# A graph layer's segment sum: one TensorE loop with an empty first pass, and a last block whose x and b2 come by products

## What is computed

```python
agg = segment_sum(edge_attr, dst, 6250)        # edge_attr 200000 x 128 fp32, dst sorted
h = relu(concat([x, agg, u[0] for every node]) @ W1 + b1)
y = h @ W2 + b2
out = layernorm(x + y)                         # 6250 x 128, over the 128 features, eps 1e-5
```

## Time and profile before

| what | value |
|---|---|
| median of three runs | 274.97 us (274.71 to 275.29) |
| the profiled execution | 274.97 us |
| its span, first to last instruction | 273.2 us |
| around the span | 1.77 us |
| TensorE / DVE / ACT / POOL busy | 78% / 64% / 19% / 15% |
| moved by DMA | 110.06 MB, mean 403 GB/s |
| mean granted TensorE clock | 0.949 of full |

### The profile page before, as it was taken

One profiled execution on the slowest core, in us unless ns is written; L12 is line 12 of the kernel. 1 busy time (PEld: TensorE's weight loads), 2 busy tenths in 40 slices (PEclk: granted clock), 3 DMA queues, 4 the chain that ended last, 5 costly groups with the idle time before them and its releaser, 6 DMA issues.

```text
span 273.2 us, 15327 instructions
## 1 busy us (share of the span) xinstructions
PE 213.4 (78%) x6767; PEld 168.1 (62%) x6767; DVE 175.8 (64%) x435; ACT 50.8 (19%) x100; POOL 40.9 (15%) x49
## 2 busy tenths in 40 slices
PE   0886899999787886875669899876797976867872
PEld 0774687877655665644557677655476755655751
DVE  7842258698874784687434867779658576465542
ACT  0410022122211211210202322212022212121210
POOL 6400010040210210310300302102004011030020
PEclk9997579999999999999779999999799999999997
DMA  7999999999999999999999999999999999999995
GB/s 245 395 396 400 400 397 404 402 402 405 401 402 403 402 405 408 417 415 418 412 405 419 419 415 418 417 419 417 424 431 423 427 426 422 427 425 421 430 396 200
DMA packets 27327, 110.06 MB, mean 403 GB/s; under 512 B 2008, under 2 KB 3374, under 8 KB 25134
## 3 DMA queue, kind: packets, MB, share of 16 engines
q1 hardware_dynamic: 24052, 105.83, 95.7%
q10 hardware_dynamic: 3258, 4.00, 4.3%
HBM read 106.63 MB, written 3.20 MB: 402 GB/s over the span
## 4 chain that ended last, share of the span: by engine, by line
PE 60%; issue 14%; DMA 13%; DVE 9%; ACT 1%; DVEq 1%; POOL 1%; POOLq 0%
PE rows_ps L868 32%; PE cols_ps L880 15%; DMA slots<-in_edge_attr 13%; PE hid_ps L894 4%; PE hid_ps L912 3%; PE hid_ps L903 3%; PE hid_ps L888 2%; ACT rows L446 1%; DVE z L680 1%; DVE tall_ids L688 1%; DVE first_of_pair L572 1%; DVE hot L617 1%; POOL rstd L410 1%; DVE dst_local L585 1%; DVE high L699 1%
## 5 line engine op out<-in xcount | busy, mean ns | idle before, releaser
L868 PE MATMUL rows_ps<-slots,hot 64*32 64x128 f32 x6240 | 112.5, 284 | 31.7 <-issue 27.5
L868 PEld LDWEIGHTS rows_ps<-slots,hot 64*32 64x32 f32 x6240 | 93.2, 110 | 48.8 <-issue 46.4
L643 DVE TENSOR_TENSOR agg_t<-agg_t,cols_ps 128x128 f32 (+1 forms) x65 | 21.1, 324 | 83.3 <-PE cols_ps L880 81.4
L880 PE MATMUL cols_ps<-row_hot,rows 128*128 128x128 f32 (+1 forms) x260 | 55.2, 337 | 14.3 <-ACT rows L446 7.3
L617 DVE TENSOR_TENSOR hot<-edge_node,iota 128x768 f32<-128x768 f32 x65 | 61.9, 952 | 2.2 <-issue 1.9
L880 PEld LDWEIGHTS cols_ps<-row_hot,rows 128*128 128x128 f32 x260 | 40.5, 199 | 28.3 <-issue 15.1
L446 ACT ACTIVATE rows<-rows_ps 128x256 f32<-128x256 f32 x65 | 24.9, 383 | 176.7 <-PE rows_ps L868 169.6
L410 POOL TENSOR_TENSOR rstd<-var_eps,minus_half 128x4 f32<-128x4 f32 (+1 forms) x13 | 15.8, 1216 | 194.6 <-DVE var_eps L674 194.6
L633 DVE TENSOR_TENSOR row_hot<-row_node,iota 128x256 f32<-128x256 f32 (+1 forms) x65 | 37.5, 576 | 0.0
L401 POOL TENSOR_TENSOR z<-x_rows,b_all 128x512 f32<-128x512 f32 (+1 forms) x13 | 17.3, 1331 | 31.5 <-PE hid_ps L888 31.5
L680 DVE TENSOR_SCALAR z<-z,moments,rstd (+1 forms) x49 | 16.6, 398 | 1.1 <-POOL rstd L410 1.0
(11 more groups left out here) (119 smaller groups left out, 70.8 us busy)
## 6 DMA issues: line engine op xcount, KB each, us to landing
slots<-in_edge_attr SPq DMA_DIRECT2D x65, 1536.0 KB, 16.8
x_rows<-in_x ACTq DMA_DIRECT2D x11, 256.0 KB
out<-z SPq DMA_DIRECT2D x11, 256.0 KB
dst_int<-in_dst ACTq DMA_DIRECT2D x1, 384.0 KB, 4.1
dst_int<-in_dst SPq DMA_DIRECT2D x1, 384.0 KB, 4.6
x_rows<-in_x ACTq DMA_DIRECT2D x1, 192.0 KB
out<-z SPq DMA_DIRECT2D x1, 192.0 KB
rest_slot<-in_edge_attr ACTq DMA_DIRECT2D x1, 128.0 KB, 8.7
```

The lines of the kernel that those rows point to most:

```text
L643: V.tensor_tensor(cols, cols, cols_ps[:, 0:n], ALU.add).then_inc(added, 1)
L868: done = T.matmul(rows_ps[i][c * SPAN:(c + 1) * SPAN, h, 0:feats], hot[j][part, c * RUN + r, :], slots[part, j, c, r * feats:(r + 1) * fea ...
L880: done = T.matmul(cols_ps[:, 0:n], rows[i][:, h, :], row_hot[j][:, h, 0:n], start=(h == 0), stop=(h == HALVES - 1))
```

## The change

TensorE has one loop for all 13 laps. Around it is a loop of two passes; in the first, `real` is 0, the lap loop runs once and every step in it is branched over, as is the preparation (`before_laps`). In every lap `level2(t-1)` comes behind `level1(t)`, but in step 4 of a lap `level2(t-1)` comes ahead of `level1(t)`, for there are only two pairs `rows_ps` and `rows` now. All `row_hot` and all sums but the last step's have 224 columns. The banks set free hold the transposed x and y apart from the hidden sums. The blocks are shifted by 128 nodes: block 0 now has the three pieces, blocks 1 to 11 are whole, and `final` is still the first 128 nodes. In the last lap, ahead of `level1` of step 64, two products place x and b2 of the final block in y's bank, and `product2` of that block adds onto them; DVE takes its statistics from that bank and normalises from there, without `residual`. The product L961 is gone. DVE has one loop for laps 1 to 11; the last lap and the ending stand twice, in the two arms of a branch on the plan, and SP's last store too. POOL clears `x_rows` at the start, and the load of x waits for that. What DVE does in laps 1 to 4 for the last steps' ids (`turn_tall_ids`) is done in laps 3 to 6.

```diff
-SETS = (0, 1, 0, 1, 2)
-DENSE_LAP = 5
-DENSE = DENSE_LAP * LAP
...
+    width = FIRST + chunks * BLOCK
+
+    top_rows = ROWS - 1
+    top_parts = nodes - FIRST - (blocks - 1) * BLOCK - top_rows * P
+    top_even = top_parts // 16 * 16
...
-        rows_ps = [pb(f"rows_ps{i}", [P, HALVES, 512]) for i in range(3)]
+        rows_ps = [pb(f"rows_ps{i}", [P, HALVES, 512]) for i in range(2)]
         cols_ps = pb("cols_ps", [P, 512])
-
+        turn_bank = pb("turn_bank", [P, BLOCK])
         hid_ps = pb("hid_ps", [P, BLOCK])
-        y_ps = hid_ps[:, :].rearrange("p (r f) -> p r f", r=ROWS)
-        turn_ps = y_ps
+        y_bank = pb("y_bank", [P, BLOCK])
+        y_ps = y_bank[:, :].rearrange("p (r f) -> p r f", r=ROWS)
+        turn_ps = turn_bank[:, :].rearrange("p (r f) -> p r f", r=ROWS)
...
             for i in range(final):
                 store(i)
             plan_now = general_if(sp)
-            store(final)
-
...
+            G.memset(x_rows[:, :, :], 0.0).then_inc(x_zero, 1)
...
+
             bias_add(0, 0)
+            bias_add(1, 1)
             for i in range(places):
                 reciprocal_deviation(i, i)
-                if i + 1 < places:
-                    bias_add(i + 1, i + 1)
+                if i + 2 < places:
...
-                    act.dma_start(x_rows[:, 0, :], x_first).then_inc(x_in, 16)
                 else:
-                    act.dma_start(x_rows[:, :, :].rearrange("p r f -> p (r f)"), x_full[blocks - 1 - i]).then_inc(x_in, 16)
+                    act.wait_ge(x_zero, 1)
+                for memory, home in pieces_of(seq % places, x, lambda parts, r0, r1: x_rows[parts, r0:r1, :].rearrange("p r f -> p (r f)")):
+                    act.dma_start(home, memory).then_inc(x_in, 16)
...
                 for j in range(LAP):
                     t = lap * LAP + j
-
-                    if dense_lap:
+                    if t:
                         copy_rows(t)
-                    elif t + 1 < DENSE:
-                        copy_rows(t + 1)
-                    if j == 0 and lap:
-                        relu(lap - 1)
-                    elif j == 3:
+                    if j == 1:
+                        if lap:
+                            relu(lap - 1)
                         copy_x(lap)
-                    elif j == 4 and lap < final:
+                    elif j == 3 and lap < final:
...
-                    with dve.If(t < DENSE):
-                        make_row_hot(t, i, False)
-                    with dve.If(t > DENSE - 1):
-                        make_row_hot(t, i, True)
-                else:
-                    n = DENSE_COLS if dense_step else COLS
-                    V.tensor_tensor(row_hot[i][:, :, 0:n],
-                                    row_node[:, bass.ds(t, 1), :].rearrange("p o h -> p (o h)").unsqueeze(2).broadcast_to([P, HALVES, n]),
-                                    iota[:, 0:n].unsqueeze(1).broadcast_to([P, HALVES, n]), ALU.is_equal).then_inc(row_hot_made, 1)
-
...
-                        if j == 2:
-                            residual(lap - 1, lap - 1)
-                        elif j == 3:
-                            variance(lap - 1, lap - 1)
-                        elif j == 4:
-                            normalise(lap - 1, lap - 1)
-                    make_hot(t + AHEAD, j + AHEAD, None if mixed else False)
-                    if not isinstance(lap, int) and j in turned_at:
+                    if j == 0 and looped:
+                        with dve.If(lap == JUDGE + 1):
+
+                            dve.wait_ge(bad_summed, 1)
+                            dve.wait_ge(level2_done, t + 1)
+                            V.tensor_copy(bad_total[:, :], bad_ps).then_inc(bad_read, 1)
+                            dve.wait_ge(bad_read, 1)
+                    add(t, at[j + 1], COLS)
+                    if j == 1:
+                        residual(lap - 1, lap - 1)
+                        if looped:
+                            with dve.If(lap == TURN + TILES):
+                                bring_tall_ids()
+                            with dve.If(lap == JUDGE):
+                                judge()
+                    elif j == 2:
+                        variance(lap - 1, lap - 1)
+                        if looped:
+                            with dve.If(lap == JUDGE + 1):
+                                make_plan()
+                    elif j == 3:
...
+            first_at = step_bases(0, LAP - 1)
+            for t in range(LAP - 1):
+                add(t, first_at[t], COLS)
+                make_hot(t + AHEAD, t + AHEAD)
+            dve.wait_ge(wide_ids_copied, SHARE)
 
             dve.wait_ge(first_in, 16)
             V.tensor_copy(edge_node[:, held, :, :].rearrange("p c r -> p (c r)"), first_int[:, :])
-            with dve.Fori(DENSE_LAP, laps) as lap:
-                dense_lap(lap)
-            residual(final, final)
-            variance(final, final)
-            normalise(final, final)
+            with dve.Fori(1, laps - 1) as lap:
+                one_lap(lap, counts(lap), range(-1, LAP - 1))
+            last_at = step_bases((laps - 1) * LAP - 1, LAP)
+            one_lap(laps - 1, last_at, range(-1, 0))
+
+            def ending():
+                one_lap(laps - 1, last_at, range(0, LAP - 1))
+
+                add(held, 0, DENSE_COLS)
+
+                dve.wait_ge(y_done, final + 1)
+                V.bn_stats(stats[:, 0, :], y_ps[:, 0, :]).then_inc(stats_made, 1)
+                joined(final, 1)
+                dve.wait_ge(z_ready, final + 1)
+                dve.wait_ge(rstd_made, final + 1)
+                V.tensor_scalar(row(final, 0), y_ps[:, 0, :], moments[:, 0, 0:1], rstd[:, 0:1], ALU.subtract, ALU.mult).then_inc(normed, 1)
...
+            plan_now = general_if(dve)
+            with dve.If(plan_now < 1):
+                ending()
                 general()
+            with dve.If(plan_now > 0):
+                ending()
 
         @block.tensor
...
+            def turn_x(seq, landed, in_laps):
+
                 pe.wait_ge(x_in, landed)
+                def more():
+                    for r in range(1, ROWS):
+                        T.transpose(turn_ps[:, r, :], x_rows[:, r, :], ident[:, :])
+                if in_laps:
+                    with pe.If(seq < final):
+                        more()
+                else:
+                    more()
+                T.transpose(turn_ps[:, 0, :], x_rows[:, 0, :], ident[:, :]).then_inc(x_turned, 1)
+
...
+            def product2(seq, i, onto=False):
+                pe.wait_ge(hid_made, seq + 1)
 
                 pe.wait_ge(z_made, seq + 1)
                 for r in range(rows_of(i)):
+                    done = T.matmul(y_ps[:, r, :], hid[:, r * P:(r + 1) * P], w2_sb[:, :], start=not onto, stop=True)
                 done.then_inc(y_done, 1)
...
-            def sparse_lap(lap):
+            def one_lap(lap, real):
                 counts(lap)
                 for j in range(LAP):
-                    t = lap * LAP + j
-                    level1(t, lap, j)
-
-                    if j:
-                        level2(t - 1, j - 1, False)
-                    else:
-                        with pe.If(lap > 0):
-                            level2(t - 1, LAP - 1, False)
-                        with pe.If(lap < 1):
-                            first_products()
-                    if j == 1:
-                        with pe.If(lap > 0):
-                            finished(lap)
-                            product1_agg(lap - 1, start_of(lap - 1))
-                    elif j == 2:
-                        with pe.If(lap > 0):
-                            product2(lap - 1, lap - 1)
-                    elif j == 4:
-                        turn_x(lap, lap, lap * 16 + 16)
-
-            def dense_lap(lap):
-                counts(lap)
-                for j in range(LAP):
-                    t = lap * LAP + j
-                    if j == 4:
-                        with pe.If(lap == JUDGE + 1):
-
-                            pe.wait_ge(plan_made, 1)
-                        with pe.If(lap > final - 1):
-                            product1_x(final, final)
...
-                        with pe.If(lap < final):
-                            product1_agg(lap - 1, start_of(lap - 1))
-                        with pe.If(lap > final - 1):
-                            product1_agg(short, 0)
-                    elif j == 1:
+                    with pe.If(real > 0):
+                        one_step(lap, j)
+
+            def one_step(lap, j):
+                t = lap * LAP + j
+                if j == 4:
+
+                    level2(t - 1, j - 1, COLS)
+                    with pe.If(lap > final - 1):
+
+                        pe.wait_ge(z_made, final + 1)
+                        T.matmul(y_ps[:, 0, :], x_t[:, 0:P], ident[:, :], start=True, stop=False)
+                        T.matmul(y_ps[:, 0, :], ones[0:1, :], b2_row[:, :], start=False, stop=False)
```

(97 more changed lines are left out.)

224 lines of the change are left out of this document (94 added, 130 removed).

## The result

The changed kernel takes 287.99 us (six runs, 286.85 to 290.67) against 275.05 (274.71 to 275.62): 5.0% slower, ratio 1.0501, 95% interval 1.0474 to 1.0528. The prediction was 275.3, at most 276.5.

What follows compares the result with a forecast made beforehand. DMA bytes bound the middle, so only the start of `level1` of step 64 and the chain behind it move the time. Order +0.84, chain −0.32, bandwidth −0.20 on 274.97 gave 275.3 us, range 274.2 to 276.5.

Steps and rivals of the forecast that it cites:

- the start: Before the first products: the empty pass might make `level1(0)` some us late, yet cost nothing up to 3 us.
- the blind sum: Whole kernel: 0.84 − 0.32 − 0.20 = +0.32 on 274.97, so 275.3 us.
- The lateness: Start of TensorE: four code fetches of 2.4 cost 9.6 us, making it some 2 to 3 late.
- the cover: First steps: the queue of loads hides TensorE's lateness, no loss while the first step is not over 3 us late.
- The margin behind it: Tightest point before, load 8 at 34.19: some 3 us ahead of an empty queue.
- The sign named beforehand: Sign of a wrong forecast: DMA share under 0.95 anywhere before 260, meaning the queue of loads ran empty.
- The page's rule: Empty pass: a taken branch to code outside TensorE's held window forces a fetch, one at every step before the first product.
- the change doesn't do what it says: Early laps: the empty pass keeps no code and stops remain; 275.5, or over 276 if first steps are late; chance 0.12.
- the order costs nothing: Last lap: `level1(64)` starts when its load lands; 274.4, or 274.1 with the whole bandwidth gain; chance 0.32.
- The order in the last lap: `level1(63)` to `level1(64)`: 4.51 against 3.67 before, so +0.84; bounds 4.3 and 5.1.
- The chain behind `level1(64)`: Ending after the last `level1`: without `residual`, statistics start 0.32 earlier, so −0.32, with 0.1 either way.
- The second rival: `level2(64)` behind the loops' exit: TensorE stops if its code is missing; 277.3, or 276.1 with half the stop; chance 0.14.

Runs made afterwards that it cites:

- The table: Kernel of before with TensorE's first product made to wait for load 0, 1, 2 or 4: 275.59, 277.36, 280.88, 289.90 us.
- the cleanest comparison: Kernel of before with only the placing of the final block's x and b2 added, in two gaps, and no `residual`: 274.90 us, ratio 1.0001.

## Why the prediction was wrong

**The step that failed is the start.** The prediction said of the empty pass: "with a stop of 2.4 each, as the trace has it, four would cost 9.6 us from the start on and make TensorE some 2 to 3 late, which the queue of loads still covers". The number four was right, the price was not: the four blocks ahead of the first product put it off by 26.80 − 5.27 = 21.5 us, 5.4 each. A block's price was taken from the longest stop, which is this row of TensorE's timeline before:

```profile
27.26 1.06 PE L868 MATMUL rows_ps<-slots,hot 64*32 64x128 f32 x19 [2.38 <-issue]
```

But from the end of the stop before it, 20.23, to the end of this one it takes 7.0 us, of which TensorE stood 2.4; the rest went by under products. A stop is what is left of a block's way behind them. In the empty pass there is no work to lie beside a block. The whole way of a block was in the trace of before, as the distance of the packets on TensorE's instruction queue in the first lap: 17.68, 24.77, 31.10, 37.55, so 6.3 to 7.1 us. With 6.5 a block the blind sum would have had a first product at 5.27 + 4 × 6.5, some 31 us.

**The lateness was mis-sized too, by its own numbers.** 9.6 us for the four blocks became "some 2 to 3 late". The kernel of before that waits for load 1 is just this case: its first product comes 9.6 us later, `level1(0)` 7.2 later, so only 2.4 are made up for, and the time is 2.4 us longer. Even with the stop's price the forecast would have left its range: 275.3 + 2.4 = 277.7, an estimate, as that kernel keeps its stops in the laps.

**The next failure is the cover.** "Nothing at either end, while the first step isn't over 3 us late" holds roughly: 2.33 late cost 0.6, no more than runs spread. The margin behind it was misread: load 8 went out at 34.19, but load 7 landed at 40.1, 5.9 us later and not some 3. Past the 3 us I had no price at all, and counted the case in which "the first steps come later than the 3 us" as "over 276", chance 0.05. The table gives 14.9 for 19.3. The sign named beforehand came: the DMA share fell under 0.95 ahead of 260.

**The page's rule pointed the right way, and I argued it away.** That a taken branch to code not held forces a fetch (the Trainium skill, "Runtime: NRT & Kernel Launch", Instruction fetch mechanics) is what the traces agree with: five packets of 16 KB for the five steps branched over, and in the kernel with one branch a single packet ahead of the first product. It spoke against the change, and what I set against it was the wrong price.

**What held.** The empty pass does keep the code: no packet from 27 us to the end of the last lap, and 416 GB/s from 118 to 145. That rival, that the change doesn't do what it says, falls. So does the first, that the order costs nothing: `level1(64)` came 4.76 behind `level1(63)`, 1.0 behind the landing of its load. The later steps could be checked with the empty pass taken out. There the sum was 275.3 and the measure 275.85 (275.62 in the profiled execution). The order in the last lap was right in kind and short in size: 4.76 against 4.51, as the placing took 279.18 − 278.45 = 0.73 where 0.44 was counted, inside the upper bound. (The lower bound, 4.3, was added up wrongly: without the placing the terms make 4.07.) `level1(63)` started 0.2 earlier than before (260.53 against 260.73), by the loads, as taken. The chain behind `level1(64)` was 0.25 shorter in the cleanest comparison, for 0.32. These two, 0.25 and 0.07, are all that the sum lacks to the profiled execution, 275.62. The early stretches do lose something: 338 GB/s for 344 in the first 20 us, and 380 from 40 to 50, where before had 403 over 40 to 105; 10 × 23/403 is 0.6 us. But the laps behind make it good, as load 63 lands 0.2 earlier than before. Why the queue runs low early is only argued: `level1(4)` now waits for `level2(3)` in a lap that still has its stops for code.

**The second rival**, code at the exit of the loops, didn't come: in the kernel without the empty pass the last `level2` starts 0.44 behind the start of the copy (266.94, then 267.38), and in the changed kernel 0.43 behind it (280.83, then 281.26), as before.

## What to carry to other kernels

A stop for code that shows in a trace is only what work did not cover; before code is read ahead by an empty run, price each block at the distance between the packets of the instruction queue, in the DMA traffic of that moment, and multiply by the blocks. Then ask what the late engine releases: here a buffer whose load keeps the DMA engines fed. The loads in line cover a small lateness; past that the time grows, in the end by more than a microsecond for each one. No run here shows a place where an empty run pays: even with the loads held back, the kernel took 288.44.

## What the runs showed that I had not expected

A block of 16 KB of TensorE's code took 3.2 us to come with DMA engines nearly idle and 5.9 with loads on them, though its packet itself lasts about 1 us. A late start costs little at first and more than one for one at the end: 9.0 us of time for the last 7.5 of lateness. A load that stands alone takes 6.4 us, where loads in line land 3.9 apart, so the DMA engines lose time before their queue is empty. And two of the three kernels without the empty pass spread more than before: 275.5 to 277.9 and 275.2 to 277.8, against 274.0 to 275.6; why stays open.
